# A post-LN decoder layer on one core: every engine's hand-written order of steps replaced by another, PSUM turns in other banks

## Chip, cores, metric

One core of one Trainium2 chip runs the whole kernel. The metric is the device time of that core in microseconds (us); three runs of the kernel before are given.

## What is computed

64 sequences of 128 tokens with 512 features go through one decoder layer: self-attention, cross-attention and a linear layer on fp8-rounded data, each added to its input and layer-normed.

```python
x = _layernorm(x + _L0_attn_ref(x, Wqkv, q_norm_w, k_norm_w, Wo))     # 16 heads of 32; rmsnorm of q and k, rope,
                                                                      # causal softmax, @ Wo
x = _layernorm(x + _L0_xattn_ref(x, ctx, ctx))                        # 8 "heads" of 16 token rows: scores are
                                                                      # 512x512 (features x features), softmax
x = _layernorm(x + _L0_ffn_ref(x, weight))                            # blocks of 128 scaled to fp8 e4m3 and back,
                                                                      # weights too, then x @ weight.T
```

## The kernel before

One batch is one sequence, a tile of 128 tokens by 512 features. The work on a batch is cut into named steps. Five engines run them: TensorE (PE), VectorE (DVE), ScalarE (ACT), GpSimd (POOL) and SyncE (SP), which issues every DMA. Nothing is scheduled at run time: for each engine a table written out by hand (`SP_STEPS`, `POOL_STEPS`, `ACT_STEPS`, `DVE_STEPS`, `PE_STEPS`, L178 to L231) gives the order. An entry `name:k@stage` is part k of a step; in slot t the engine does it for batch t - stage. A slot is one pass through the table, so some six batches are in flight at once: the self-attention of one batch, the cross-attention of earlier ones, the linear layer of a still earlier one. Slots of an engine are its own; engines meet only by semaphores. The stage is therefore partly a name: `ld_x:0@0` and `ld_x:0@1` differ in which slot of SP holds them, not in the batch that comes next.

`LAST` is the highest stage of all tables. The first `LAST + 3` slots and the last ones are written out (unrolled); the others run in a hardware loop (`Fori`, two slots per round, so that double buffers have fixed addresses).

PE's steps in the order of one batch: `x_T` (transpose x), `proj_q/k/v` (each four parts of three matmuls: the operand is split into a high part `lin_h` and a low part `lin_l`, and high x high, high x low, low x high are summed), `parts_T` (transposed q and k), `self_scores` (for the row maximum), `self_shift_T`, `self_scores_T`, `self_pv`, `proj_o`; then `context_T`, 32 `cross_scores` (for the maximum) into two PSUM banks `mx`, `cross_shift_T`, 32 `cross_scores_T` into two banks `st`, 8 `cross_pv` into bank `pv`, `group_T`, `back_T`; then `quant_T` and `ffn`.

For these DVE does `cross_max` (one for each of the 32 `cross_scores`, of which PE may be two ahead), `self_max`, `self_shift`, `cross_shift`, `rope_terms`, `self_recip` and `self_norm`, `cross_norm`, the sums `add_self`, `add_cross`, `add_ffn`, `layernorm` and the low parts `xT_low`, `oT_low`, `xdT_low`. ACT does `probs` (exp of each `cross_scores_T`, again two ahead at most), `self_probs`, `self_stack`, `context_out`, `group_out`, `part_high` and the high parts `xT_high`, `oT_high`, `xdT_high`. POOL does `quant_unit` and `quant_round`, `layer_rstd`, `mask`, `rope_sum`, `part_low`, `query_low`, `mean_square`, `context_rest`. The row maxima of the cross-attention go as a shift through DRAM: `cross_shift_T` (PE), `cross_shift_out` (ACT), `st_sh2` and `ld_sh2` (SP, L413 and L420), and `cross_scores_T:0` and `:16` wait for the load.

All results of PE other than these go into three shared PSUM banks. `BANK` (L235) gives each kind of result, a "turn", its bank. Turns of one bank follow each other in PE's order: a turn waits (`before`) until the one ahead of it in the same bank has been read out, which the reader says by `bank_free`. `full` and `freed` are the points at which a turn is written or read out.

`lin_h` and `lin_l` exist once, and the three linear layers (q, k and v together; o; ffn) use them in turn. Nothing in the code before makes the writer of `lin_h` wait until the layer ahead has been read; the order of the tables does it.

Of the kernel before, what the change touches and what calls it, by code (L numbers as in the profile page):

```python
# [5 lines left out]
def post_ln_decoder_kernel(nc, x, ctx_in, wqkv, q_norm_w, k_norm_w, wo, wffn, cos_t, sin_t, out):  # L6
# [52 lines left out]
    with es:  # L59
# [127 lines left out]
        ACT_STEPS = steps("""
            probs:4@4 self_stack:2@1 probs:5@4 probs:6@4 probs:7@4 self_stack:3@1 probs:8@4 probs:9@4
            context_out:0@3 probs:10@4 probs:11@4 probs:12@4 probs:13@4 probs:14@4 xdT_high:0@5
            context_high:0@2 probs:15@4 xT_high:0@0 cross_shift_out:1@4 query_high:0@2 group_out:0@4  # L190
            square:0@0 self_shift_out:0@1 context_high:1@2 probs:16@4 square:1@0 part_high:0@0
            probs:17@4 probs:18@4 probs:19@4 value:0@0 self_probs:0@1 probs:20@4 self_probs:1@1
            probs:21@4 probs:22@4 self_probs:2@1 probs:23@4 self_probs:3@1 probs:24@4 probs:25@4
            self_stack:0@0 probs:26@4 probs:27@4 cross_shift_out:0@3 probs:28@4 probs:29@4 probs:30@4
            probs:31@4 part_high:1@0 oT_high:0@1 group_out:1@4 self_stack:1@0 probs:0@3 probs:1@3
            probs:2@3 probs:3@3""")
        DVE_STEPS = steps("""
            layernorm:1@5 quant_scale:0@5 add_self:0@2 quant_magic:0@5 cross_max:22@4 cross_max:23@4
            self_max:0@1 cross_max:24@4 cross_max:25@4 cross_max:26@4 cross_max:27@4 cross_max:28@4
            cross_max:29@4 xdT_low:0@5 self_max:1@1 cross_max:30@4 cross_max:31@4 self_max:2@1  # L200
            cross_shift:1@4 layernorm:0@2 cross_max:0@3 xT_low:0@0 add_ffn:0@5 self_max:3@1
            layernorm:2@5 cross_max:1@3 self_shift:0@1 cross_max:2@3 rope_terms:0@0 cross_max:3@3
            cross_max:4@3 cross_max:5@3 cross_max:6@3 cross_max:7@3 cross_max:8@3 rope_terms:1@0
            cross_max:9@3 cross_max:10@3 cross_max:11@3 cross_max:12@3 cross_max:13@3 cross_max:14@3
            cross_max:15@3 cross_shift:0@3 self_recip:0@1 self_recip:1@1 self_recip:2@1 self_recip:3@1
            cross_max:16@3 self_norm:0@1 cross_max:17@3 cross_norm:0@4 oT_low:0@1 cross_max:18@3
            cross_norm:1@4 cross_max:19@3 add_cross:0@4 cross_max:20@3 cross_max:21@3""")
        PE_STEPS = steps("""
            proj_o:3@2 context_T:0@3 cross_scores_T:5@4 cross_scores_T:6@4 cross_pv:0@4
            cross_scores_T:7@4 parts_T:3@1 cross_scores_T:8@4 cross_scores:23@4 self_scores:0@1  # L210
            cross_scores_T:9@4 cross_pv:1@4 cross_scores_T:10@4 cross_scores:24@4 cross_scores:25@4
            cross_scores_T:11@4 self_scores:1@1 cross_scores_T:12@4 cross_scores:26@4 self_scores:2@1
            cross_scores:27@4 cross_scores_T:13@4 cross_scores_T:14@4 cross_scores:28@4 quant_T:0@5
            cross_scores:29@4 cross_scores_T:15@4 cross_pv:2@4 cross_scores:30@4 cross_scores:31@4
            ffn:0@5 ffn:1@5 ffn:2@5 ffn:3@5 x_T:0@0 cross_shift_T:1@4 cross_scores:0@3 cross_pv:3@4
            self_scores:3@1 cross_scores:1@3 proj_q:0@0 proj_q:1@0 proj_q:2@0 proj_q:3@0
            cross_scores:2@3 proj_k:0@0 proj_k:1@0 self_shift_T:0@1 proj_k:2@0 cross_scores:3@3
            proj_k:3@0 cross_scores_T:16@4 cross_scores:4@3 proj_v:0@0 cross_scores_T:17@4
            cross_scores:5@3 cross_scores_T:18@4 cross_scores:6@3 proj_v:1@0 cross_scores:7@3
            proj_v:2@0 cross_scores:8@3 cross_scores_T:19@4 cross_scores:9@3 cross_scores_T:20@4  # L220
            proj_v:3@0 self_scores_T:0@1 cross_pv:4@4 cross_scores:10@3 self_scores_T:1@1
            cross_scores_T:21@4 cross_scores:11@3 cross_scores_T:22@4 self_scores_T:2@1
            cross_scores:12@3 self_pv:0@1 cross_scores:13@3 cross_scores_T:23@4 self_pv:1@1
            self_scores_T:3@1 cross_scores:14@3 cross_scores_T:24@4 cross_scores:15@3
            cross_scores_T:25@4 self_pv:2@1 parts_T:0@0 self_pv:3@1 cross_scores_T:26@4
# [850 lines left out]
```

## Time and profile before

| | us |
|---|---|
| median of 3 runs | 3355.27 |
| lowest, highest | 3353.78, 3358.29 |
| the profiled execution, span | 3353.3 |

| engine | busy us | share |
|---|---|---|
| PE matmul | 3148.0 | 94% |
| PE weight load | 1676.5 | 50% |
| DVE | 2792.0 | 83% |
| ACT | 2093.1 | 62% |
| POOL | 1251.8 | 37% |

The busy shares are even over the whole span except the first and the last tenth. PE's records overlap (a matmul is recorded with its way through the array), so its busy share says little of how full it is; distances between starts say more. The DMA queues move 66 GB/s on the mean and their packets take 21% of the time of the 16 engines.

### The profile page before, as it was taken

What the parts mean: (1) busy time and instruction counts of PE and PEld (TensorE: products, weight loads), DVE (VectorE), ACT (ScalarE), POOL (GpSimd) and SP (SyncE); (2) the same over time, 40 slices, a digit from 0 to 9 for tenths busy, and PEclk for the clock granted to TensorE, in tenths of its full rate; (3) what the DMA queues carried; (4) which work ended last, traced back from release to release, by engine and by line L of the source; (5) the groups of instructions that cost most, each with busy time, mean ns of one, the idle gap of its engine ahead of it and who ended that gap; (6) DMA issues with size and microseconds to landing.
All of it is one profiled execution on the core that took longest, in us unless ns stands there. A gap on an engine that the chain in (4) does not pass through costs nothing.

```text
span 3353.3 us, 79176 instructions
## 1 busy us (share of the span) xinstructions
PE 3148.0 (94%) x22224; PEld 1676.5 (50%) x22224; DVE 2792.0 (83%) x5187; ACT 2093.1 (62%) x3905; POOL 1251.8 (37%) x1623
## 2 busy tenths in 40 slices
PE   1689999999999999999999999999999999999986
PEld 1445555555555555555555555555555555555432
DVE  6368888888888888888888888888888888888874
ACT  0346666666676666666667666666666766666653
POOL 3223334334343333433433333343343433334321
PEclk9789999999999999999999999999999999999997
DMA  2022222222222222222222122222222222222220
GB/s 75 26 62 74 71 67 71 63 72 65 70 73 64 72 64 66 71 63 73 64 70 73 63 71 66 66 71 63 71 66 70 73 63 71 65 66 71 67 64 17
DMA packets 203973, 220.66 MB, mean 66 GB/s; under 512 B 37760, under 2 KB 160640, under 8 KB 203776
## 3 DMA queue, kind: packets, MB, share of 16 engines
q1 hardware_dynamic: 203776, 218.77, 21.4%
q14 instruction: 163, 1.34, 0.1%
q8 instruction: 34, 0.56, 0.1%
HBM read 141.57 MB, written 77.07 MB: 65 GB/s over the span
## 4 chain that ended last, share of the span: by engine, by line
PE 75%; DVE 14%; issue 7%; POOL 2%; ACT 1%; DVEq 1%; DMA 1%; SPq 0%; POOLq 0%; ACTq 0%
PE bank L872 19%; PE mx L985 14%; PE st L1002 13%; PE pv L1014 12%; PE bank L865 5%; PE bank L907 3%; DVE nm L715 3%; PE bank L956 3%; DVE st L776 2%; PE bank L939 2%; PE bank L959 2%; DVE lin_l L743 1%; DVE yout L838 1%; PE bank L923 1%; PE bank L920 1%
## 5 line engine op out<-in xcount | busy, mean ns | idle before, releaser
L715 DVE TENSOR_REDUCE nm<-mx 128x1 f32<-128x512 f32 x2048 | 1355.0, 685 | 219.9 <-PE mx L985 210.2
L559 ACT ACTIVATE pp<-st 128x512 f32<-128x512 f32 x2048 | 1153.0, 597 | 400.9 <-PE st L1002 385.1
L985 PE MATMUL mx<-kst,qst 96*128 96x512 bf16 x2048 | 765.4, 387 | 29.2 <-DVE nm L715 28.8
L1002 PE MATMUL st<-qst,kst 98*128 98x512 f16 x2048 | 739.6, 387 | 6.9 <-DMA qst<-cross_shift 2.6
L1014 PE MATMUL pv<-pp,vT 128*32 128x512 f32 x4096 | 551.2, 610 | 0.0
L985 PEld LDWEIGHTS mx<-kst,qst 96*128 96x128 f16 x2048 | 189.1, 98 | 445.5 <-DVE nm L715 283.1
L872 PE MATMUL bank<-w_h,lin_h 128*128 128x512 f32 x768 | 394.0, 513 | 4.5 <-DVE lin_l L743 4.4
L1002 PEld LDWEIGHTS st<-qst,kst 98*128 98x128 bf16 x2048 | 190.7, 98 | 317.8 <-ACT pp L559 216.6
L490 POOL TENSOR_SCALAR rstd<-mv 128x1 f32<-128x1 f32 x192 | 36.9, 192 | 817.2 <-DVE mv L779 812.1
L872 PE MATMUL bank<-w_l,lin_h 128*128 128x512 f32 x768 | 306.0, 398 | 0.0
L872 PE MATMUL bank<-w_h,lin_l 128*128 128x512 f32 x768 | 305.0, 397 | 0.0
L500 POOL TENSOR_TENSOR qkn<-ropeA,qkn 128x512 f16<-128x512 f32 x128 | 148.4, 1159 | 397.2 <-ACT qkn L581 391.4
L763 DVE RECIPROCAL o<-bank 128x128 f32<-128x128 f32 x256 | 217.1, 910 | 42.8 <-PE bank L959 42.7
L506 POOL TENSOR_SCALAR_AFFINE_SELECT p<-p 128x512 f32<-128x512 f32 x256 | 163.4, 638 | 197.8 <-ACT p L616 197.7
L496 POOL TENSOR_TENSOR ropeA<-ropeA,ropeB 128x512 f32<-128x512 f32 x128 | 163.7, 1279 | 144.9 <-DVE ropeB L755 144.9
L574 ACT ACTIVATE junk<-bank 128x512 bf16<-128x512 f32 x128 | 76.1, 594 | 203.3 <-PE bank L872 203.3
L616 ACT ACTIVATE p<-bank 128x512 f32<-128x512 f32 x256 | 152.6, 596 | 56.1 <-PE bank L939 47.4
L729 DVE TENSOR_REDUCE nm<-bank 128x4 f32<-128x512 f32 x256 | 174.6, 683 | 10.4 <-PE bank L923 10.3
L568 ACT ACTIVATE lin_h<-bank 128x512 fp32r<-128x512 f32 x64 | 38.2, 597 | 221.1 <-PE bank L865 221.1
L907 PE MATMUL bank<-ident,qkn 128*96 128x128 f16 x2048 | 161.9, 223 | 14.4 <-DVE o L763 7.2
L872 PEld LDWEIGHTS bank<-w_h,lin_h 128*128 128x128 f32 x768 | 149.4, 195 | 44.8 <-DVE lin_l L743 5.9
L907 PEld LDWEIGHTS bank<-ident,qkn 128*96 128x96 f16 x2048 | 146.0, 125 | 48.4 <-issue 19.3
(131 smaller groups left out, 5417.6 us busy)
## 6 DMA issues: line engine op xcount, KB each, us to landing
qst<-q_planes SPq DMA_DIRECT2D x640, 64.0 KB, 2.2
kst<-k_planes SPq DMA_DIRECT2D x640, 64.0 KB, 2.2
k_planes<-kpl SPq DMA_DIRECT2D x64, 384.0 KB, 2.6
xb<-x SPq DMA_DIRECT2D x64, 256.0 KB, 2.7
cx<-ctx SPq DMA_DIRECT2D x64, 256.0 KB, 3.3
...
```

The lines of the kernel that those rows point to most:

```text
L496: g_.tensor_tensor(ropeA[:], ropeA[:], ropeB[:], ALU.add).then_inc(s_rope, 1)
L506: g_.affine_select(out=p1[c % 2][:], in_=p1[c % 2][:], compare_op=ALU.is_ge, fill=0.0, base=0, pattern=[[0, HC], [1, P]], channel_multipli ...
L559: a.activation(pp[:, unit % 2, j, :], st[n % 2][:], ACT.Exp, scale=CROSS_SCALE).then_inc(st_free, 1)
L715: v.tensor_reduce(nm2[:, n // 16, n % 16:n % 16 + 1], mx[n % 2][:], AX.X, ALU.max, negate=True)\
L729: v.tensor_reduce(nm1[:, HC * c:HC * (c + 1)], at(f"s1m{c}")[:].rearrange("p (h k) -> p h k", h=HC), AX.X, ALU.max, negate=True).then_inc( ...
L763: v.reciprocal(o1[:, cols], at("pvs")[:, cols]).then_inc(done, 1)
L865: last = t.transpose(dst[:, c * P:(c + 1) * P], src(c), idm[:])
L872: last = t.matmul(at(name)[:], a[:, rows], w[:, part, cols], start=(part == 0 and i == 0), stop=(part == KC - 1 and i == 2))
L907: last = t.transpose(at(name)[0:SROWS, h * P // 2:(h + 1) * P // 2].bitcast(F16), qkn[k][:, 8 * (i % 2) + h, :, :].rearrange("p g d -> p ( ...
L985: t.matmul(mx[n % 2][:], qst[b.i][0:XROWS, h, c * P:(c + 1) * P], kst[b.i][0:XROWS, h, :], start=True, stop=True).then_inc(mx_full, 1)
L1002: t.matmul(st[n % 2][:], kst[b.i][:, h, i * P:(i + 1) * P], qst[b.i][:, h, :], start=True, stop=True).then_inc(st_full, 1)
L1014: last = t.matmul(pv[32 * j:32 * j + 2 * XD, :], vT[b.i][:, i, GH * g + j, :], pp[:, unit % 2, j, :], start=(i == 0), stop=(i == KC - 1))
```

## The change

Every engine does the same steps, in another order. Some stages are renamed, on SP by one or two, so that `LAST` goes from 5 to 7: the loop begins at slot 10 instead of 8, has 26 rounds instead of 27, and the program has 71 slots instead of 69. Eleven turns have another bank. And the three steps that write `lin_h` wait, by a new function `linear_before`, until the linear layer ahead of theirs in PE's order is done. The tables, the banks and the waits after the change, cut to the parts that are spoken of:

```diff
         SP_STEPS = steps("""
-            ld_cx:0@2 ld_qst:1@3 ld_kst:0@3 ld_x:0@0 st_sh2:1@4 ld_sh2:1@4 st_out:0@5 st_qpl:0@2
-            st_sh1:0@1 ld_sh1:0@1 ld_qst:0@2 st_x2:0@2 ld_x2r:0@4 st_sh2:0@3 st_kpl:0@2 ld_sh2:0@3
-            ld_kst:1@2""")
+            st_sh2:0@5 ld_x2r:0@6 st_kpl:0@4 st_out:0@7 st_x2:0@4 st_qpl:0@4 ld_sh2:0@5 ld_kst:0@4
+            ld_qst:0@4 ld_cx:0@3 ld_x:0@1 st_sh1:0@2 st_sh2:1@5 ld_sh1:0@2 ld_sh2:1@5 ld_kst:1@4
+            ld_qst:1@4""")
...
         ACT_STEPS = steps("""
+            part_high:1@1 group_out:1@5 self_stack:1@1 probs:0@4 probs:1@4 context_out:0@3
+            probs:2@4 oT_high:0@2 probs:3@4 probs:4@4 self_stack:2@1 probs:5@4 probs:6@4 probs:7@4
+            probs:8@4 probs:9@4 probs:10@4 self_stack:3@1 probs:11@4 context_high:0@2 xdT_high:0@5
+            probs:12@4 probs:13@4 xT_high:0@0 self_shift_out:0@1 context_high:1@2
...
+            query_high:0@2 probs:25@4 self_probs:3@1 probs:26@4 probs:27@4 self_stack:0@0
+            probs:28@4 cross_shift_out:0@3 probs:29@4 probs:30@4 probs:31@4""")
         DVE_STEPS = steps("""
+            cross_norm:1@5 cross_max:24@4 self_norm:0@2 add_cross:0@5 cross_max:25@4 oT_low:0@2
+            layernorm:1@5 quant_scale:0@5 cross_max:26@4 cross_max:27@4 quant_magic:0@5
+            cross_max:28@4 cross_max:29@4 self_max:0@1 cross_max:30@4 add_self:0@2 cross_max:31@4
+            cross_max:0@3 self_max:1@1 xdT_low:0@5 self_max:2@1 cross_max:1@3 self_max:3@1
+            cross_max:2@3 self_shift:0@1 cross_shift:1@4 xT_low:0@0 cross_max:3@3 cross_max:4@3
+            add_ffn:0@5 cross_max:5@3 cross_max:6@3 layernorm:0@2 cross_max:7@3 cross_max:8@3
...
+            cross_max:17@3 cross_max:18@3 cross_shift:0@3 cross_max:19@3 layernorm:2@5
+            cross_max:20@3 self_recip:0@1 self_recip:1@1 self_recip:2@1 cross_max:21@3
+            cross_norm:0@4 self_recip:3@1 cross_max:22@3 cross_max:23@3""")
         PE_STEPS = steps("""
+            self_pv:3@2 cross_scores_T:28@5 cross_shift_T:0@4 cross_scores_T:29@5
+            cross_scores:21@4 cross_scores_T:30@5 group_T:0@5 cross_scores_T:31@5 cross_pv:6@5
+            cross_pv:7@5 cross_scores:22@4 parts_T:1@1 cross_scores:23@4 group_T:1@5
+            cross_scores:24@4 cross_scores_T:0@4 back_T:0@5 cross_scores:25@4 cross_scores_T:1@4
+            context_T:0@3 cross_scores_T:2@4 parts_T:2@1 cross_scores_T:3@4 cross_scores_T:4@4
+            parts_T:3@1 cross_scores_T:5@4 cross_scores:26@4 cross_scores_T:6@4 proj_o:0@2
...
+            ffn:0@5 ffn:1@5 ffn:2@5 x_T:0@0 ffn:3@5 cross_scores:3@3 cross_scores:4@3
+            self_shift_T:0@1 cross_pv:2@4 cross_shift_T:1@4 cross_scores_T:14@4
+            cross_scores_T:15@4 proj_q:0@0 proj_q:1@0 cross_scores:5@3 cross_pv:3@4
...
         BANK = {
+            "xT": 1, "q": 1, "k": 2, "v": 1, "tqk0": 1, "tqk1": 1, "tqk2": 2, "tqk3": 1, "s1m0": 2,
+            "s1m1": 0, "s1m2": 1, "s1m3": 0, "m1T": 0, "s1t0": 0, "s1t1": 0, "s1t2": 1, "s1t3": 1,
+            "pvo": 0, "pvs": 2, "wo": 0, "vT": 2, "mT0": 1, "mT1": 0, "o2T0": 1, "o2T1": 2, "o2N": 1,
             "xdT": 2, "ffn": 2}
...
+        LINEARS = (("proj_q", "v"), ("proj_o", "wo"), ("ffn", "ffn"))
+
+        def linear_before(name, b):
+
+            opens = [(i, stage, turn) for i, (step, k, stage) in enumerate(PE_STEPS) if k == 0
+                     for first, turn in LINEARS if step == first]
+            own = [turn for _, _, turn in opens].index(name)
+            for back in range(1, len(opens) + 1):
+                _, stage, turn = opens[own - back]
+                ahead = opens[own][1] - stage - (back > own)
+                if b.rnd is not None or 0 <= b.b + ahead < BATCH:
+                    return [full(turn, b, ahead)]
+            return []
...
             def xT_high(b, _):
+                for point in linear_before("v", b):
+                    act.wait_ge(*point)
                 act.wait_ge(*full("xT", b))
...
             def oT_high(b, _):
+                for point in linear_before("wo", b):
+                    act.wait_ge(*point)
...
             def xdT_high(b, _):
+                for point in linear_before("ffn", b):
+                    act.wait_ge(*point)
```

## Rows read from the trace of the kernel before

**Rows 1.** The page: engines with busy us and share; the chain that ended last.
```profile
PE 3148.0 (94%) x22224; PEld 1676.5 (50%) x22224; DVE 2792.0 (83%) x5187; ACT 2093.1 (62%) x3905; POOL 1251.8 (37%) x1623
PE 75%; DVE 14%; issue 7%; POOL 2%; ACT 1%; DVEq 1%; DMA 1%; SPq 0%; POOLq 0%; ACTq 0%
```

**Rows 2.** Tile lin_l, whole run and three stretches: count, durations, first and last start us.
```profile
L743 DVE TENSOR_TENSOR lin_l<-bank,lin_h x64: 680/681/692, 71.8 to 3130.2; 128x512 fp32r<-128x512 f32 x64
...
L743 DVE TENSOR_TENSOR lin_l<-bank,lin_h x20: 680/681/682, 1505.7 to 2442.0; 128x512 fp32r<-128x512 f32 x20
...
L743 DVE TENSOR_TENSOR lin_l<-bank,lin_h x4: 681/681/681, 323.8 to 468.9; 128x512 fp32r<-128x512 f32 x4
...
L743 DVE TENSOR_TENSOR lin_l<-bank,lin_h x2: 681/681/681, 1554.2 to 1604.2; 128x512 fp32r<-128x512 f32 x2
```

**Rows 3.** Stage 1500 to 1549.1 with its clock; PE timeline: start us, us, what.
```profile
1500.00:1549.10 49.10, 48.62 (x355) 25.93 (x347) 43.45 (x82) 33.09 (x64) 19.11 (x25) 1.00 0.22 68
...
1508.25 0.39 PE L872 MATMUL bank<-w_l,lin_h 128*128 128x512 f32 x1
1508.48 0.39 PE L872 MATMUL bank<-w_h,lin_l 128*128 128x512 f32 x1
...
1519.16 1.06 PE L1014 MATMUL pv<-pp,vT 128*32 128x512 f32 x8
1520.15 0.39 PE L985 MATMUL mx<-kst,qst 96*128 96x512 bf16 x1
1520.38 0.39 PE L939 MATMUL bank<-qs,ks 98*128 98x128 f16 x4
```

**Rows 4.** Timeline around `self_shift_T`, 1504 to 1512: PE, DVE, POOL.
```profile
1511.68 0.22 PE L930 MATMUL bank<-ident,sh 128*32 128x128 f16 x1 [0.48 <-DVE sh L739]
...
1509.06 1.37 DVE L784 TENSOR_SCALAR yout<-yout,mv,rstd 128x512 f32<-128x512 f32 x1 [0.44 <-POOL rstd L492]
...
1508.99 1.16 POOL L540 TENSOR_TENSOR qpl<-x,qpl 128x512 f16<-128x512 f32 x1
```

**Rows 5.** The jumps: waits, DVE and ACT timeline, instruction queue of 1480 to 1578.6.
```profile
DVE x L784 <- issue: 48.3, 26, 2.0
...
1490.42 0.55 DVE L784 TENSOR_SCALAR x<-x,mv,rstd 128x512 f32<-128x512 f32 x1 [2.03 <-issue]
...
1488.02 1.16 ACT L559 ACTIVATE pp<-st 128x512 f32<-128x512 f32 x2 [0.55 <-PE st L1002]
...
q14 instruction: 5, 0.04, 0.1%
```

**Rows 6.** SP's timeline from 1499 on; landing of the stores; first user on PE.
```profile
1528.69 0.36 SPq L413 DMA_DIRECT2D cross_shift<-sh2T  x1
1529.31 0.41 SPq L373 DMA_DIRECT2D k_planes<-kpl  x1
1530.29 0.29 SPq L420 DMA_DIRECT2D qst<-cross_shift  x1
...
cross_shift<-sh2T SPq DMA_DIRECT2D x128, 8.0 KB, 1.4
...
1534.64 0.60 PE L1002 MATMUL st<-qst,kst 98*128 98x512 f16 x2
```

**Rows 7.** DVE's timeline of 1526 to 1535.
```profile
1526.55 3.39 DVE L763 RECIPROCAL o<-bank 128x128 f32<-128x128 f32 x4 [0.49 <-PE bank L959]
...
1534.00 0.24 DVE L799 RECIPROCAL r<-bank 128x16 f32<-128x16 f32 x1
1534.27 0.43 DVE L802 TENSOR_TENSOR yq<-bank,r 128x256 f32<-128x256 f32 x1
```

**Rows 8.** ACT: `context_out` (ns min/median/max); timeline of 1525 to 1529.
```profile
L640 ACT ACTIVATE vT<-bank x64: 583/602/612, 170.7 to 3256.2; 128x512 f32<-128x512 f32 x64
...
1525.94 1.02 ACT L600 ACTIVATE qs<-bank 96x1024 f16<-96x1024 f16 x1 [0.37 <-PE bank L907]
1528.19 0.27 ACT L646 ACTIVATE sh2T<-bank 32x128 f16<-32x128 f16 x1 [0.26 <-PE bank L991]
```

More of the change, by code:

```diff
@@ L178, in post_ln_decoder_kernel @@
         SP_STEPS = steps("""
-            ld_cx:0@2 ld_qst:1@3 ld_kst:0@3 ld_x:0@0 st_sh2:1@4 ld_sh2:1@4 st_out:0@5 st_qpl:0@2
-            st_sh1:0@1 ld_sh1:0@1 ld_qst:0@2 st_x2:0@2 ld_x2r:0@4 st_sh2:0@3 st_kpl:0@2 ld_sh2:0@3
-            ld_kst:1@2""")
+            st_sh2:0@5 ld_x2r:0@6 st_kpl:0@4 st_out:0@7 st_x2:0@4 st_qpl:0@4 ld_sh2:0@5 ld_kst:0@4
+            ld_qst:0@4 ld_cx:0@3 ld_x:0@1 st_sh1:0@2 st_sh2:1@5 ld_sh1:0@2 ld_sh2:1@5 ld_kst:1@4
+            ld_qst:1@4""")
         POOL_STEPS = steps("""
-            quant_unit:0@5 quant_round:0@5 quant_round:1@5 quant_round:2@5 layer_rstd:0@2
@@ L184, in post_ln_decoder_kernel @@
-            context_rest:0@2 layer_rstd:2@5 query_low:0@2 mean_square:0@0 rope_sum:0@0 mean_square:1@0
-            part_low:0@0 context_rest:1@2 mask:0@1 mask:1@1 rope_sum:1@0 mask:2@1 mask:3@1 part_low:1@0
-            layer_rstd:1@4""")
+            quant_round:0@5 quant_round:1@5 quant_round:2@5 layer_rstd:0@2 context_rest:0@2
+            mean_square:0@0 rope_sum:0@0 mean_square:1@0 part_low:0@0 layer_rstd:2@5 mask:0@1
+            context_rest:1@2 mask:1@1 rope_sum:1@0 mask:2@1 mask:3@1 query_low:0@2 part_low:1@0
@@ L187, in post_ln_decoder_kernel @@
+            layer_rstd:1@4 quant_unit:0@4""")
         ACT_STEPS = steps("""
[L188 to L196, printed above, removed]
-        DVE_STEPS = steps("""
[L198 to L207, printed above, removed]
@@ L208, in post_ln_decoder_kernel @@
-        PE_STEPS = steps("""
[L209 to L225, printed above, removed]
-            cross_scores_T:27@4 cross_pv:5@4 cross_shift_T:0@3 cross_scores_T:28@4 cross_scores_T:29@4
-            group_T:0@4 cross_scores_T:30@4 cross_scores:16@3 cross_scores_T:31@4 cross_pv:6@4
-            cross_scores:17@3 cross_pv:7@4 cross_scores:18@3 cross_scores:19@3 parts_T:1@0 group_T:1@4
-            proj_o:0@1 cross_scores:20@3 cross_scores_T:0@3 cross_scores_T:1@3 back_T:0@4 parts_T:2@0
-            proj_o:1@1 cross_scores_T:2@3 cross_scores:21@3 proj_o:2@1 cross_scores_T:3@3
-            cross_scores:22@3 cross_scores_T:4@3""")
@@ new lines, in post_ln_decoder_kernel @@
+            part_high:1@1 group_out:1@5 self_stack:1@1 probs:0@4 probs:1@4 context_out:0@3
+            probs:2@4 oT_high:0@2 probs:3@4 probs:4@4 self_stack:2@1 probs:5@4 probs:6@4 probs:7@4
+            probs:8@4 probs:9@4 probs:10@4 self_stack:3@1 probs:11@4 context_high:0@2 xdT_high:0@5
+            probs:12@4 probs:13@4 xT_high:0@0 self_shift_out:0@1 context_high:1@2
+            cross_shift_out:1@4 probs:14@4 probs:15@4 group_out:0@4 square:0@0 self_probs:0@1
+            probs:16@4 probs:17@4 square:1@0 part_high:0@0 probs:18@4 probs:19@4 probs:20@4
```

18 lines of the change are left out of this document (added), and 3 rows, old and new, of the table BANK.

## The prediction

> **What bounds the kernel now.** I read the page first. TensorE (PE) is busy in 94% of the span and carries 75% of the chain that ended last, VectorE (DVE) 14% [rows 1]. A busy PE is not a full one, so the next view is the pace: the instruction at L743 (`xT_low`) runs once for each batch, so the distance between two of them is one period. All 64 give (3130.2 - 71.8)/63 = 48.55 us; inside the hardware loop 20 of them give (2442.0 - 1505.7)/19 = 49.28 us; in the unrolled slots ahead of it four of them give (468.9 - 323.8)/3 = 48.37 us [rows 2]. The kernel is 71.8 us of start, 63 periods, and 223 us from the last L743 to the end.
>
> How full is PE in a period? I take the distance from one start to the next where nothing waits. A linear matmul costs 0.23 us, a scores matmul 0.22, a `cross_pv` 0.99 plus 0.09 ahead of it [rows 3]. In the same way, from the PE rows of one period, a block of four transposes costs 0.44, `parts_T` 0.45, `self_pv` 0.67, `self_scores` 0.44, `self_scores_T` 0.22, a shift transpose 0.15. A period has 60 linear matmuls (14.0), 64 scores (14.1), 8 `cross_pv` (8.7), 6 transpose blocks (2.6), 4 each of `parts_T`, `self_pv`, `self_scores`, `self_scores_T` (7.1), 3 shifts (0.5): 47.0 us. The granted clock of the stretch is 1.00, the level of 2.4 GHz [rows 3]. So 49.28 is a floor of 47.0 plus 2.3 us of waits. The change keeps every step, so the floor stays, and the question is only which waits go and which come.
>
> **What the change removes.** (a) `self_shift_T` stands behind `proj_k:1`. PE arrives 0.75 us too early: the shift on DVE stands behind `add_ffn` and `layernorm:2`, which waited for POOL and took 1.37 us instead of 0.55 because POOL's `query_low` ran beside it [rows 4]. In the new order `self_shift` stands well ahead of `add_ffn` and `self_shift_T` behind `ffn:3` and two scores; it is early by about 1 us. Gain 0.75 a period. (b) Once in two slots DVE jumps back to the head of its loop: 2.03 us of idle with nothing awaited, 26 such, 48.3 us in all. ACT's jump falls between two `probs` at 1488.02 and costs nothing [rows 5]. DVE's jump makes PE late by the difference of 50.0 and 48.5 us that neighbouring L743 show [rows 2], 0.7 a period. The instruction queue loads 5 blocks in two periods [rows 5]. Counted over the trace's instructions, its loads come after every 128 instructions of an engine, and these 5 are all DVE's: DVE's body of the loop (291 instructions) lay over four such blocks, ACT's (336) over three, and only the engine with four reloads. LAST goes from 5 to 7, so the loop begins at slot 10 and the bodies move. Counting the two more unrolled slots from the tables, I estimate that DVE's body comes to lie on three blocks and ACT's, by 11 instructions, on four: the reload goes over to ACT. (c) `group_T:0` waits 0.25 for `cross_shift_out:0` today; in the new order it does so no more.
>
> The Trainium skill (Runtime: NRT & Kernel Launch, section Instruction fetch mechanics) says that a taken branch whose target has left the window of resident blocks waits for a fetch. That agrees with the idle of DVE in the trace; without this rule only the estimate of which engine pays next would be missing.
>
> **What it adds.** I walk the new PE table at floor pace, from the start of `self_pv:3` at 0: `cross_scores_T:28` 0.58, `cross_shift_T:0` 0.80, T30 1.39, `cross_pv:7` 3.45, `group_T:1` 5.34, `cross_scores_T:0` 6.00, `back_T` 6.22, `context_T` 7.09, `parts_T:2` 7.75, `proj_o:0` 9.56.
>
> (d) `cross_scores_T:0` needs `ld_sh2:0`. On ACT `self_stack:0` (1.02) and `probs:28` stand ahead, so `cross_shift_out:0` (0.27) ends at 1.75 [rows 8] and `st_sh2:0` starts at 1.95. On SP it was followed by one other DMA and then `ld_sh2:0`, 1.60 us behind; now five stand between (`ld_x2r`, `st_kpl`, `st_out`, `st_x2`, `st_qpl`), and one unblocked DMA follows another after 0.62 us [rows 6], or somewhat more where, as for `ld_x2r` and `ld_sh2`, it has two waits. So `ld_sh2:0` is issued at about 1.95 + 6 x 0.68 = 6.0. Its landing is not shown; the store of the same 8 KB lands after 1.4, and today PE uses it 4.35 us after the issue without waiting for it [rows 6]. I take 1.6, near the store's: T0 at 7.6 instead of 6.0, `back_T` at 7.8 instead of 6.22. Bounds for the wait: 1.2 (DVE's chain, next) to 2.5.
>
> (e) `back_T` also needs the DVE chain: three `self_recip` from 0.71 on (0.82 to 0.88 each), `cross_max:21` (a `cross_max` keeps DVE 0.6), `cross_norm:0`, `self_recip:3`, `cross_max:22`, `:23`, `cross_norm:1` [rows 7]: 0.71 + 2.5 + 0.6 + 0.67 + 0.82 + 1.2 + 0.75 = 7.3. Today 9.2 us of PE work lie over this chain, then 6.2. It is 1.15 late, beside (d) and not added to it. Together with 0.25 at T30, which waits for `probs:28`, (d) and (e) give 1.6.
>
> (f) `parts_T:2` now takes the bank that `context_T` has just filled: transposes 0.60, `context_out` 0.60 [rows 8], two hand-overs, 1.3 us where PE has 0.66 of work. Wait 0.65 (bounds 0.6 and 0.9). Behind it PE's whole queue stands.
>
> (g) T3 to T6 follow at 0.2 to 0.5 us while ACT, at 0.5 a `probs`, also has `context_out`, `oT_high` and `self_stack:2`: 0.3 (bounds 0 and 0.6).
>
> (h) ACT's reload, 3.0 us from branch to work as on DVE, stands ahead of `part_high:1` and `group_out:1`; `group_T:1`, `cross_norm:1`, `back_T` follow at 9.05 instead of 7.8: 1.25 in two slots, 0.6 a period (bounds 0 and 1.3).
>
> (i) The three waits for the preceding linear layer: `xT_high` now waits for `ffn:3`, which follows `x_T` at once. ACT gets going at 24.0 by the new table, `xT_low` ends 1.5 us later, and `proj_q` comes at 25.55 with `self_shift_out` and `context_high:1` queued behind on ACT, neither needed within 1 us: nothing. `oT_high` waits for a `proj_v` and `xdT_high` for a `proj_o` that are over: nothing; from below 0, from above 0.2 if ACT is late.
>
> One rule speaks about (e). The row first: `layernorm:2` took 1.37 us, until 0.28 after `query_low` had ended [rows 4]. The Trainium skill (SBUF — State Buffer, section SBUF: two separate sides) calls the port pair of VectorE and GpSimd an exclusive lock held for a whole instruction. In the new order `layernorm:2` stands just ahead of the `self_recip`s and again meets `query_low`. By my walk it gets free 0.1 us before they can start; were it later by the whole 0.8, (e) would give 7.3 + 0.7 and only draw level with (d). So the sum is the same by the one and by the other.
>
> **Sum.** New slot: 47.0 + 0.3 (the small waits left) + 1.6 + 0.65 + 0.3 = 49.85, in the loop 50.45 with (h). Loop: 52 slots x (50.45 - 49.28) = +61. Two slots move from the loop to straight code: 2 x (49.85 - 49.28) = +1. About five full slots outside: 5 x (49.85 - 48.37) = +7. Start and end keep their chains. Against the profiled execution of 3353.3 (median of the runs 3355.3, 2 us more): 3355 + 69 = 3424.
>
> **Rivals.** R1, faster: `ld_sh2:0` lands early enough that (e) alone sets `back_T`, ACT's reload is hidden, and (g) is nothing. Slot 47.0 + 1.2 + 0.65 = 48.85 with none of the small waits left: 52 x -0.43 + 5 x 0.5 = -20, 3335. It decides at a `ld_sh2:0` issued under 4 us after `st_sh2:0`. For it: (a) and (b) are sure gains of 1.4. Against: five issues at 0.62 or more. Chance 0.19. R2, nothing to measure: ACT pays no reload and (d) is nearer 1.2 than 1.6: 49.4 in all slots, 3355 + 6 = 3361. Chance 0.08. R3: as forecast but without (h): 52 x 0.57 + 8 = +38, 3393. Chance 0.18. R4: both reloads remain, DVE's ahead of `cross_norm:1` where no cover is: another 0.6 a period, 3455. Chance 0.08. That the change doesn't do what it says can't be: the tables are the program. My forecast has 0.47.
>
> **Numbers.** Differences under 0.2% (7 us) can't be told from none. Faster 0.19 (R1), same 0.08 (R2), slower 0.73. The range runs from R1's end to R4's, 3335 to 3455.
>
> **What would show it.** L743 spacing of about 49.9 and 51 us in turn; at `cross_scores_T:0` a PE wait for the DMA from the shift's scratch; at `parts_T:2` (L907) one for ACT's L640; `self_shift_T` without a wait; DVE's 2 us idle of "issue" gone and one like it on ACT. Wrong would be: spacing under 49.3, or no wait at L1002 for a DMA. Then SP's five DMAs are cheaper than these rows say, or the walk sets two waits side by side that are one.

## The result and the profile after

The changed kernel takes 3645.6 us (median of 4 runs, 3638.0 to 3648.2), the kernel before 3355.3: a ratio of 1.086, interval 1.084 to 1.088, 290 us slower. The profiled execution is 3642.2 us long. The forecast was 3424.

Below, from the page of the kernel after: engines, granted clock (in 40 slices), the two instruction queues (loads, MB, share), the chain by engine.

```profile
PE 3220.9 (88%) x22224; PEld 1706.6 (47%) x22224; DVE 2813.1 (77%) x5187; ACT 2103.5 (58%) x3905; POOL 1249.0 (34%) x1623
...
PEclk9999999999999999999999999999999999999998
...
q8 instruction: 265, 4.34, 0.5%
q14 instruction: 162, 1.32, 0.1%
...
PE 76%; issue 9%; DVE 5%; SPq 3%; DMA 3%; ACT 3%; POOL 1%; ACTq 0%; DVEq 0%; POOLq 0%
```

Against [rows 1], PE has 73 us more of busy time for the same 22224 matmuls, and "issue", an engine waiting for nothing the profile shows, rose from 7% to 9%. The line that the prediction did not use is q8, the instruction queue of PE: 265 loads of 16 KB, where the page of before has 34. q14, with the other engines' loads of 8 KB, has nearly as many as before (162, then 163).

The pace, as in [rows 2], is now read at L765 (the same `xT_low`): the whole run, a stretch in the loop, one ahead of it.

```profile
L765 DVE TENSOR_TENSOR lin_l<-bank,lin_h x64: 684/692/693, 71.7 to 3422.3; 128x512 fp32r<-128x512 f32 x64
...
L765 DVE TENSOR_TENSOR lin_l<-bank,lin_h x43: 691/692/692, 676.6 to 2994.3; 128x512 fp32r<-128x512 f32 x43
...
L765 DVE TENSOR_TENSOR lin_l<-bank,lin_h x4: 692/692/692, 259.9 to 410.3; 128x512 fp32r<-128x512 f32 x4
```

Outside the loop a slot takes (410.3 - 259.9)/3 = 50.1 us, 0.3 over the forecast of 49.85. Inside it takes (2994.3 - 676.6)/42 = 55.2, against 50.45. So some 5 us a slot arise only in the loop, where 0.6 were forecast. The 50.1 comes near the walk's sum by two errors that nearly cancel (below, under the floor).

PE's rows with the waits of the whole run (engine, line, releaser: us, times, longest), and both engines' rows with "issue":

```profile
PE bank L978 <- issue: 93.5, 25, 4.8
...
PE st L1024 <- DMA qst<-cross_shift: 57.9, 39, 2.2
PE bank L887 <- ACT o L580: 42.2, 27, 2.7
PE bank L929 <- ACT vT L660: 32.1, 62, 0.8
ACT qkn L598 <- issue: 31.4, 11, 4.1
PE mx L1007 <- issue: 25.9, 25, 1.8
```

L978 is `self_pv`, the first thing behind PE's branch: 25 stalls of 3.7 us with nothing awaited, one at each of the 25 jumps back. In each round a second one of 1.0 us follows some 3 us later, at a `cross_scores` (L1007). L1024 is the forecast wait of `cross_scores_T:0` for the shift's DMA, L929 that of `parts_T:2` for `context_out`. DVE's row of 26 stalls of 1.9 us in the mean [rows 5] is gone, and ACT has one in its place, at `part_high:1` (L598). `self_shift_T` (L952) has no row any more.

Two neighbouring slots of the loop, as in [rows 3] (us of window; busy PE, PEld, DVE, ACT, POOL; granted clock; DMA), then the timelines of PE and ACT behind the branch of the next round:

```profile
1471.80:1525.60 53.80, 50.52 (x347) 26.74 (x351) 41.85 (x78) 32.27 (x61) 19.07 (x25) 0.94 0.20 64
1525.60:1580.60 55.00, 48.34 (x358) 25.82 (x350) 44.56 (x83) 33.26 (x62) 19.07 (x25) 1.00 0.20 62
```

```profile
1580.59 0.66 PE L978 MATMUL bank<-p,va 128*32 128x128 f32 x8 [3.69 <-issue]
...
1581.60 0.61 PE L1024 MATMUL st<-qst,kst 98*128 98x512 f16 x1
...
1591.58 0.38 PE L1024 MATMUL st<-qst,kst 98*128 98x512 f16 x1
...
1589.10 0.63 ACT L598 ACTIVATE qkn<-ropeA 128x512 f16<-128x512 f32 x1 [2.58 <-issue]
```

A stall of 3.69 us; behind it the scores matmul takes 0.61 us where it takes 0.38 ten us later: the clock's lower level, 1.2 GHz, granted after the idle (0.50 from 1580.7 to 1587.4, 1.00 on both sides of it). Where a slot's mean clock is 0.94, such stretches are in it. ACT's stall of 2.58 follows in the same slot.

Last, the term (d), SP's queue and the waiting scores matmul, as in [rows 6]:

```profile
1527.69 0.35 SPq L429 DMA_DIRECT2D cross_shift<-sh2T  x1
...
1531.16 0.74 SPq L448 DMA_DIRECT2D q_planes<-qpl  x1
1532.31 0.28 SPq L436 DMA_DIRECT2D qst<-cross_shift  x1
...
1534.57 0.39 PE L1024 MATMUL st<-qst,kst 98*128 98x512 f16 x1 [1.79 <-DMA qst<-cross_shift]
```

The load is issued 4.62 us behind the store (forecast: 4.1), its user starts 2.26 behind the issue and had waited 1.79 (forecast: 1.6).

### The profile page after: what moved, and what is told of

It reads as the page before. It is cut to its first block, busy times and chain, and to the rows that moved or that the text cites. A ratio compares the mean times of both kernels' runs of the same rounds, so it can differ in the third digit from the quotient of the medians.

```text
span 3642.2 us, 78580 instructions
## 1 busy us (share of the span) xinstructions
PE 3220.9 (88%) x22224; PEld 1706.6 (47%) x22224; DVE 2813.1 (77%) x5187; ACT 2103.5 (58%) x3905; POOL 1249.0 (34%) x1623
## 4 chain that ended last, share of the span: by engine, by line
PE 76%; issue 9%; DVE 5%; SPq 3%; DMA 3%; ACT 3%; POOL 1%; ACTq 0%; DVEq 0%; POOLq 0%
PE bank L894 25%; PE st L1024 13%; PE mx L1007 11%; PE pv L1036 11%; PE bank L887 4%; PE bank L929 3%; DMA qst<-cross_shift 2%; PE bank L978 2%; PE bank L942 2%; PE bank L981 2%; PE bank L945 2%; PE bank L961 2%; DVE x L813 1%; ACT vT L660 1%; SPq L448 1%
## 5 line engine op out<-in xcount | busy, mean ns | idle before, releaser
L575 ACT ACTIVATE pp<-st 128x512 f32<-128x512 f32 x2048 | 1168.5, 597 | 689.1 <-PE st L1024 501.9
L1024 PE MATMUL st<-qst,kst 98*128 98x512 f16 x2048 | 795.4, 404 | 67.6 <-DMA qst<-cross_shift 57.9
L1007 PE MATMUL mx<-kst,qst 96*128 96x512 bf16 x2048 | 789.3, 391 | 37.2 <-issue 25.9
L1036 PE MATMUL pv<-pp,vT 128*32 128x512 f32 x4096 | 561.7, 633 | 3.2 <-ACT pp L575 3.2
L894 PE MATMUL bank<-w_h,lin_h 128*128 128x512 f32 x768 | 402.9, 525 | 6.3 <-DVE lin_l L765 4.7
L1024 PEld LDWEIGHTS st<-qst,kst 98*128 98x128 bf16 x2048 | 196.6, 100 | 417.6 <-ACT pp L575 202.7
L1007 PEld LDWEIGHTS mx<-kst,qst 96*128 96x128 f16 x2048 | 195.8, 98 | 409.5 <-issue 266.0
L498 POOL TENSOR_SCALAR rms<-ssq 128x1 f32<-128x1 f32 x128 | 24.5, 191 | 801.1 <-ACT junk L592 800.9
L785 DVE RECIPROCAL o<-bank 128x128 f32<-128x128 f32 x256 | 225.0, 920 | 90.9 <-PE bank L981 90.9
L929 PE MATMUL bank<-ident,qkn 128*96 128x128 f16 x2048 | 166.4, 227 | 57.1 <-ACT vT L660 32.1
L929 PEld LDWEIGHTS bank<-ident,qkn 128*96 128x96 f16 x2048 | 147.9, 128 | 126.9 <-issue 53.3
L978 PE MATMUL bank<-p,va 128*32 128x128 f32 x2048 | 110.6, 289 | 95.8 <-issue 93.5
L1036 PEld LDWEIGHTS pv<-pp,vT 128*32 128x32 f32 x4096 | 91.6, 112 | 177.6 <-issue 87.1
```

The source lines that it names most:

```text
L575: a.activation(pp[:, unit % 2, j, :], st[n % 2][:], ACT.Exp, scale=CROSS_SCALE).then_inc(st_free, 1)
L785: v.reciprocal(o1[:, cols], at("pvs")[:, cols]).then_inc(done, 1)
L894: last = t.matmul(at(name)[:], a[:, rows], w[:, part, cols], start=(part == 0 and i == 0), stop=(part == KC - 1 and i == 2))
L929: last = t.transpose(at(name)[0:SROWS, h * P // 2:(h + 1) * P // 2].bitcast(F16), qkn[k][:, 8 * (i % 2) + h, :, :].rearrange("p g d -> p ( ...
L978: last_v = t.matmul(at("pvo")[HD * j:HD * (j + 1), cols], va[b.i][:, HC * c + j, :], p1[c % 2][:, j, :], start=True, stop=True)
L1007: t.matmul(mx[n % 2][:], qst[b.i][0:XROWS, h, c * P:(c + 1) * P], kst[b.i][0:XROWS, h, :], start=True, stop=True).then_inc(mx_full, 1)
```

## The experiments

Each compares with the kernel before on the same chip (3353.7 to 3357.9 in these sets). The waits put in ahead of an engine's first slot are on a semaphore that has long been raised; two such waits make one instruction, so a loop over 129 in place of one wait gives 64 instructions more. Where they delay the start, the first `xT_low` shows by how much, and I take that off.

**Moving the bodies.** e1, the changed kernel with 64 more instructions on PE, nothing changed in the body:

```
-            pe.wait_ge(u_done, 1)
+            for _ in range(129):
+                pe.wait_ge(u_done, 1)
```

> The changed kernel with 64 satisfied waits put ahead of TensorE's first slot, so that its loop body of 1583 instructions lies 64 instructions further on; nothing inside the body differs. Theory (the position of the body decides): in the changed kernel TensorE's instruction queue loads 9 blocks of 16 KB in each of the 26 rounds and the pair of slots takes 109.3 us, where two slots outside the loop take 100.2. Moved on by 64, the body lies over one block fewer, the loads inside the loop go (some 35 to 40 in all, from 265), and a slot in the loop takes about 50.1 + 0.6 (ScalarE's own reload) = 50.7 us: 3645 - 52 x 4.0 = 3437 us, between 3415 and 3460. Rival (the new order or the new banks cost this inside the loop only, through a wait that needs the steady state): nothing of the order is touched, so 3645 +- 10 us and 109 us per round.

3544.5 us (ratio 1.055, 1.053 to 1.057), 40 loads on q8, no "issue" row for `self_pv` (L979 there). The start was delayed by 7.0 us, so the reload of PE, with what follows from it, costs 101 + 7 = 108 us, 4.2 in each of 26 rounds, half of what I had expected: moving the body stops the reload, and its price had been set at twice its size. What was left over pointed at ACT. The waits, two slots:

```profile
ACT qkn L598 <- issue: 48.2, 20, 2.6
...
PE bank L888 <- ACT o L580: 35.6, 28, 1.7
```

```profile
1340.20:1393.90 53.70, 50.75 (x355) 27.30 (x351) 43.07 (x81) 32.60 (x62) 19.12 (x25) 0.94 0.21 63
1393.90:1446.40 52.50, 49.84 (x355) 26.78 (x348) 43.01 (x81) 32.94 (x62) 19.10 (x25) 0.97 0.21 64
```

e4, the same and 30 more instructions on ACT (`for _ in range(61)`):

> The first of these kernels with 30 satisfied waits ahead of ScalarE's first slot as well: ScalarE's body of 334 instructions then lies over three blocks of 128, not four. Theory (term h): the 2.7 to 4.5 us at ScalarE's branch falls to 0.3, which gives 1.2 us in two slots: 26 x 1.2 = 32 us below the kernel with the 64 waits alone, about 3405 us if that one takes 3437. Rival (ScalarE has slack at its branch and the reload costs nothing): the same time as that kernel within 0.2%.

3484.4 us (1.039, 1.035 to 1.044), 60 below e1: 2.3 us a round, twice the forecast 1.25. The direct part is the row of L888 above, `group_T:1` waiting for `group_out` 35.6 us in 28 times, 1.3 each; that row is gone in e4. The rest I put down to the clock: in e1 both slots above are under 1.00, in e4 most slots take 50.9 us and have 1.00, and the mean granted clock of the whole run rises from 0.957 to 0.973.

e3, the kernel before with 40 more instructions on DVE:

> The kernel before with 40 satisfied waits ahead of VectorE's first slot: its body of 291 instructions then lies over three blocks of 128, not four. Theory (terms b and the rule of four blocks in the prediction): the 2.0 us at VectorE's branch falls to about 0.3 as on GpSimd and SyncE, 5 loads per round go, and what it cost the path, 0.7 us in each slot of the loop, goes with it: 3355 - 54 x 0.7 = 3318 us, between 3305 and 3335. Rival (the path waits for something else at that place, or other waits take it over): within 0.2% of 3355 though the loads go. Second rival (the position does not decide): the branch still takes 2 us.

3313.9 us (0.987, 0.985 to 0.988), 42.9 below the kernel before; forecast by term (b): 38. q14 falls to 33 loads, DVE's 26 stalls are gone, and all slots of the loop take 48.5 us, but one. Three slots, and PE's timeline in the middle one:

```profile
550.00:598.00 48.00, 47.52 (x347) 25.60 (x346) 42.47 (x80) 32.40 (x61) 19.12 (x25) 1.00 0.23 69
598.00:653.00 55.00, 51.24 (x349) 27.16 (x349) 43.02 (x81) 32.78 (x61) 19.08 (x25) 0.94 0.21 62
653.00:702.00 49.00, 48.47 (x350) 26.32 (x349) 43.27 (x82) 32.77 (x62) 19.11 (x25) 1.00 0.23 69
```

```profile
603.25 0.77 PE L873 MATMUL bank<-wo_h,lin_h 128*128 128x512 f32 x1 [3.28 <-issue]
603.82 0.63 PE L873 MATMUL bank<-wo_l,lin_h 128*128 128x512 f32 x1
```

There, in one round, PE reloaded in the order of before too: 9 loads more (43 on q8, not 34), a stall of 3.28 us behind the branch at 599.46, matmuls of 0.63 us instead of 0.40 after it, and a slot 6.3 us longer than its neighbours. So the reload is not bound to the changed order. It also shows that PE's place alone does not decide: e3 leaves PE's body where the kernel before has it.

**Where does PE reload?** If the body's place decides, the kernel before must be brought to do it. e2 and e5, before with 222 and 233 more instructions on PE:

> The kernel before with 222 satisfied waits ahead of TensorE's first slot: its body of 1581 instructions moves to where, in 256s, that of the changed kernel lies. Theory (position): 9 blocks per round for each of 27 rounds, some 280 loads instead of 34, and 7 to 8 us more per round, as in the changed kernel: 3355 + 27 x 7.6 + some us for the waits themselves = 3565 us, between 3530 and 3600. Rival (the order and the banks of the changed kernel are what costs): only the waits themselves, 3355 to 3370 us, and no load inside the loop.

> The kernel before with 233 satisfied waits ahead of TensorE's first slot: its body now begins at 130 of 256, exactly where that of the changed kernel does (the 222 of the run before put it at 119, where nothing was reloaded). Theory (position alone decides whether TensorE reloads): 9 blocks in each of 27 rounds, some 280 loads in all, and per round what the changed kernel paid beyond its copy moved by 64, (3645.6 - 3544.5 + 10 for the 64 waits) / 26 = 4.3 us: 3357 + 23 for the waits themselves + 27 x 4.3 = 3495 us, between 3450 and 3530. Rival (the changed kernel reloads by something of its own order, such as how far its front end runs ahead): no load in the loop and 3380 us as with 222.

3379.6 and 3381.5 us, 35 loads each, none in the loop; the first L743 came 24 and 25 us late, which is all the difference. My theory fell in this form, although with 233 the body lay where that of the changed kernel does. Mended, it was tried with e9 (22 more), e12 and e13 (the changed kernel with 24 and 245 more), e14 and e16 (before with 245 and 5 more):

> The kernel before with 22 satisfied waits ahead of TensorE's first slot: its body of 1581 instructions then begins at 175 and branches at 219, counted in 256s of the profiled instructions. Theory, mended after the runs with 222 and 233: what decides is whether TensorE fetches one more block before it reaches its branch. The loads seen in straight-line code fall at 163 to 220 of 256 in all kernels; in the changed kernel the last one fell 13 instructions ahead of the branch in the first round of the loop, and every later round reloaded; in the kernel before it would fall about at the branch (once it fell 9 ahead, and that round reloaded), and with 222 and 233 it falls behind the branch. With 22 it falls some 20 to 45 instructions ahead in each round: 9 loads in each of 27 rounds, and 3357 + 3 for the waits + 27 x 4.3 = 3476 us, between 3430 and 3510. Rival (the reload belongs to the changed kernel's order, not to where the body lies): 3360 us and no load in the loop.

> The changed kernel with 24 satisfied waits ahead of TensorE's first slot, not 64. In it TensorE runs on for 20 instructions behind its branch and then stalls 3.5 to 3.8 us for the next block, so a block ends 20 instructions into the body; 24 further on, that border lies ahead of the body, which then touches 7 blocks and not 8. Theory (a body that touches 8 blocks can reload, one of 7 can not): some 40 loads, no stall, 3645 - 101 - some us, near 3545. Rival (only a shift that is far enough, or the timing at the branch, stops it): 265 loads and 3645 us.

> The changed kernel with 245 satisfied waits ahead of TensorE's first slot: the body starts 11 instructions earlier in its block than in the changed kernel (245 = 256 - 11), so it still touches 8 blocks, with its branch some 15 instructions into the eighth. Theory (8 blocks in the changed kernel's order reload): some 265 loads in all and 3645 + 25 to 35 us for the waits. Rival (the reload of the changed kernel hangs on the exact place at which its branch lies in the eighth block): about 40 loads and 3545 + 30 us.

> The kernel before with 245 satisfied waits ahead of TensorE's first slot: its body starts some 12 instructions ahead of the border of a block and touches 8 blocks, with the branch some 35 into the eighth. With none, 222, 233 and 22 waits it did not reload. Theory (the same as for the changed kernel: 8 blocks, and the branch far enough in the eighth that one more block is asked for first): 9 loads per round and 3357 + 25 + 27 x 4.3 = 3500 us. Rival (in this order the ninth block is not asked for before the branch, wherever the branch lies): 35 loads and 3382 us.

> The kernel before with 5 satisfied waits ahead of TensorE's first slot. Of the changed kernel's four places two reloaded (branch at 176 and 200 of 256) and two did not (165 and 240); of six places of the kernel before none did (163, 174, 186, 219 and, twice, 197), but for one round at 197. Theory (one more block is fetched before the branch, if the branch lies far enough behind the border of a block, and only while the body's start lies ahead of that border; 197 is just short of it in this order): at 202 some or all of the 27 rounds reload, each for 4 to 6 us: 3358 + 27 x 5 = 3490 us if all do. Rival (nothing of this order brings the reload on): 3358 us and 34 loads.

The table gives where the branch at the body's end lies among the instructions of PE in the trace, counted from the first and modulo 256 (a 16 KB load is 256 of them).

| kernel | more instructions | branch at | q8 loads | us |
|---|---|---|---|---|
| after | 0 | 176 | 265 | 3645.6 |
| after (e12, one run) | 24 | 200 | 265 | 3698.9 |
| after (e1) | 64 | 240 | 40 | 3544.5 |
| after (e13, one run) | 245 | 165 | 41 | 3575.4 |
| before (e2) | 222 | 163 | 35 | 3379.6 |
| before (e5) | 233 | 174 | 35 | 3381.5 |
| before (e14, one run) | 245 | 186 | 35 | 3384.2 |
| before | 0 | 197 | 34 | 3355.3 |
| before (e16, one run) | 5 | 202 | 34 | 3360.1 |
| before (e9) | 22 | 219 | 34 | 3357.4 |

In the changed kernel it goes by the place: the same body reloads at two places and not at two others. The waits that move the body also delay PE's start (by 7 us in e1), and the two were not tried apart. e13, less the 27 us by which its start is late, is 3548.5, where e1 less its 7 is 3537.5. e12 is dearer than the kernel after: its second stall in a round is 2.5 us and not 1.0.

```profile
PE bank L979 <- issue: 89.3, 25, 3.9
...
PE bank L982 <- issue: 63.3, 25, 3.0
```

```profile
975.80:1027.00 51.20, 48.46 (x353) 26.19 (x352) 43.45 (x81) 32.72 (x61) 19.08 (x25) 1.00 0.22 67
1027.00:1087.00 60.00, 51.35 (x346) 26.39 (x346) 43.01 (x81) 32.80 (x61) 19.06 (x25) 0.91 0.19 57
```

In the kernel before none of six places brought it on, save the one round of e3. e12's expectation (a body that touches 7 blocks can't reload) was wrong, and so were those of e9, e13, e14 and e16. One thing goes with it: in after and e12 a load begins 0.0 to 0.5 us ahead of 47 of the 52 branches, and 0.2 to 0.8 us behind the other five; in e3's one round it begins 0.95 ahead. Where nothing reloads, none begins less than 2.4 us ahead of a branch. That looks like one block more fetched just ahead of the branch, in the place of one that the body's start still needs; it is argued, not shown. What makes PE fetch it in one order and not in the other at like places stays open.

**The forecast waits.** With the reloads of PE and ACT away, what is left of the change can be tried by itself. e6 is e4 with the load directly behind its store:

```
-            st_sh2:0@5 ld_x2r:0@6 st_kpl:0@4 st_out:0@7 st_x2:0@4 st_qpl:0@4 ld_sh2:0@5 ld_kst:0@4
+            st_sh2:0@5 ld_sh2:0@5 ld_x2r:0@6 st_kpl:0@4 st_out:0@7 st_x2:0@4 st_qpl:0@4 ld_kst:0@4
```

> The changed kernel without reloads (64 waits on TensorE, 30 on ScalarE: 3484 us) and ld_sh2:0 directly behind st_sh2:0 on SyncE, where five other steps lie between. Theory (term d: the first transposed scores of the new batch wait 1.5 to 2 us for that load, behind five DMAs, and TensorE's clock falls after that wait in some slots): the wait falls to nothing, back_T then waits up to 1.2 us for VectorE's chain (term e), the slot falls from 50.9 to 49.9 to 50.4, and the slots of 52 to 55 us with a low clock go (0.5 us a slot in the mean): 3484 - 64 x 1.1 = 3414 us, between 3380 and 3450. Rival (that wait ends by the store's and load's own latency, or the other five steps now come late): 3484 +- 10 us.

3389.9 us (1.010, 1.008 to 1.012), 94.5 below e4: better than the middle of my range. First e4: the wait's row, two slots, PE in the slower one; then e6: `cross_scores_T:0` with `back_T` behind it, and the spacing:

```profile
PE st L1026 <- DMA qst<-cross_shift: 98.3, 63, 2.7
```

```profile
1383.80:1434.70 50.90, 48.17 (x359) 25.80 (x351) 43.01 (x81) 32.84 (x62) 19.11 (x25) 1.00 0.22 65
868.30:923.10 54.80, 52.33 (x356) 28.63 (x348) 43.10 (x81) 33.06 (x62) 19.12 (x25) 0.91 0.20 61
```

```profile
877.05 0.61 PE L1026 MATMUL st<-qst,kst 98*128 98x512 f16 x1 [1.58 <-DMA qst<-cross_shift]
877.45 1.06 PE L889 MATMUL bank<-ident,yq 128*128 128x128 f32 x4
```

```profile
1448.31 0.38 PE L1026 MATMUL st<-qst,kst 98*128 98x512 f16 x1
1449.38 0.63 PE L889 MATMUL bank<-ident,yq 128*128 128x128 f32 x4 [0.70 <-DVE yq L825]
```

```profile
L766 DVE TENSOR_TENSOR lin_l<-bank,lin_h x47: 691/692/692, 668.4 to 2969.9; 128x512 fp32r<-128x512 f32 x47
```

The DMA's wait of 98.3/63 = 1.56 us is gone; `back_T` now waits 0.70 for DVE, which is term (e) come to light behind (d), as forecast. The slot falls from 50.9 to (2969.9 - 668.4)/46 = 50.03. And the slots of 52 to 55 us are gone: in e4 they had a clock of 0.91 to 0.97; right behind the wait the transposes took 1.06 us, in e6 0.63, in some slots and not in others with like waits. So the wait cost 0.85 us a slot by itself and in the mean of the loop another 0.5 by the clock.

e7 is e4 with `"vT": 0` in place of 2:

> The changed kernel without reloads (3484 us) and the turn vT in bank 0, where the kernel before had it, not in bank 2 just ahead of the third parts_T. Theory (term f): the 0.6 to 0.7 us for which parts_T:2 waits for context_out in each slot goes, and nothing else is late there: 3484 - 64 x 0.65 = 3442 us, between 3425 and 3460. Rival (proj_o:0, whose turn is in bank 0 too, then waits for context_out or self_norm in its place): 3484 +- 10 us.

3478.3 us (1.038, 1.035 to 1.040), 6 below e4, within the scatter of both. The wait left its place:

```profile
PE st L1026 <- DMA qst<-cross_shift: 102.1, 63, 3.0
...
PE st L1026 <- ACT pp L576: 29.9, 116, 0.7
```

The row of `parts_T:2` for `context_out` (32.5 us in 62 in e4) is not there any more, and PE waits 29.9 us for ACT's exponentials, 116 times, where e4 has 4.8 us in 15. So ACT holds PE up at this place with the bank or without.

e11 is e6 with `back_T:0` behind `cross_scores_T:2`, four steps later; e15 is e11 with `oT_low:0` ahead of `add_cross:0` on DVE:

> The changed kernel without reloads and with ld_sh2:0 forward (3390 us), and back_T four steps later on TensorE, behind cross_scores_T:2. Theory (term e: back_T waits 0.86 us for VectorE's chain; term f: parts_T:2 waits 0.7 us for context_out): in the new place VectorE is ready, and back_T's own 0.44 us covers part of the wait behind it: 50.03 - 0.86 - 0.4 = 48.8 us a slot, 3390 - 64 x 1.2 = 3313 us, between 3300 and 3340. Rival (ScalarE's exponentials, which run late in the same stretch, take the place of both waits, as they did when vT changed its bank): 3390 to 3375 us.

> The changed kernel without reloads, ld_sh2:0 forward and back_T later (3398 us), with VectorE's oT_low ahead of add_cross, where it stood behind it. In the kernel of 3398 us the waits of back_T and parts_T:2 were gone and proj_o:0 waited 0.8 to 1.1 us for oT_low, which stood behind add_cross, which waits for back_T. Theory (VectorE's order of these two hands the wait on): proj_o:0's wait goes and the slot falls from 50.1 to 49.2: 3398 - 64 x 0.9 = 3340 us, between 3325 and 3365. Rival (VectorE's chain is late as a whole, or ScalarE's oT_high is): 3398 +- 10 us.

3398.5 (1.013, 1.011 to 1.015) and 3476.7 us (1.036, 1.035 to 1.038). Neither gained. The waits of e11 first, then of e15:

```profile
PE bank L896 <- DVE lin_l L796: 43.5, 62, 0.8
```

```profile
PE mx L1009 <- DVE nm L738: 78.4, 80, 2.2
...
PE bank L931 <- DVE x L832: 73.8, 60, 1.3
...
DVE lin_l L796 <- ACT lin_h L642: 79.1, 64, 2.5
```

In e11 `proj_o:0` waits for `oT_low`, which stands behind `add_cross`, which waits for `back_T`. In e15 `parts_T:3` waits for `add_cross` (L832 ends the turn of `back_T` in its bank) and PE for `cross_max` (L738), for `oT_low` itself waits 1.2 us for ACT's `oT_high` in each slot (L796; 4.2 us in all in e11) and holds up DVE's queue. I read this as one chain through PE, DVE and ACT that is late at this place in all three orders (e6, e11, e15); no run takes it away.

**Parts on the kernel before.** e8 is e3 with `self_shift_T` alone moved:

```
-            cross_scores:2@3 proj_k:0@0 proj_k:1@0 self_shift_T:0@1 proj_k:2@0 cross_scores:3@3
+            cross_scores:2@3 proj_k:0@0 proj_k:1@0 proj_k:2@0 cross_scores:3@3 self_shift_T:0@1
```

> The kernel before with VectorE's 40 waits (3314 us) and self_shift_T two steps later on TensorE, behind proj_k:2 and cross_scores:3. Theory (term a alone): the wait of 0.48 us for self_shift and what follows from it, 0.75 us in each slot, goes, as self_shift's result is there 1.1 us before it is asked for: 3314 - 60 x 0.75 = 3269 us, between 3260 and 3290. Rival (proj_v:0, which needs the same bank, waits for self_shift_out instead): 3314 +- 7 us or slower.

3283.7 us (0.978, 0.977 to 0.980): the fastest kernel of this study, 30 below e3 and 74 below the kernel before. The rival fell. The slot went from 48.5 to (2964.2 - 659.8)/48 = 48.0 us: the wait of 0.48 in [rows 4] went and nothing came in its place. The 0.27 that I had added for what follows from it did not.

e10 is e8 with the three waits for the preceding linear layer and 90 more instructions on ACT:

> The kernel of 3284 us (before, 40 waits on VectorE, self_shift_T later) with the changed kernel's waits of xT_high, oT_high and xdT_high for the preceding linear layer added to its own order, and with 90 satisfied waits ahead of ScalarE's first slot so that its longer body does not come to lie over a fourth block. Theory (term i): the preceding linear layer has ended 3 us and more before each of these copies, so the waits cost nothing: 3284 +- 8 us. Rival (a copy comes later, and the linear layer behind it on TensorE too): 0.3 us or more in each slot, 3304 us or more.

3290.2 us (0.981, 0.979 to 0.983), 6.5 more. All of it lies in the start and the end; the slots are the same:

```profile
L765 DVE TENSOR_TENSOR lin_l<-bank,lin_h x64: 680/681/692, 77.8 to 3065.4; 128x512 fp32r<-128x512 f32 x64
```

```profile
L744 DVE TENSOR_TENSOR lin_l<-bank,lin_h x64: 680/681/692, 72.8 to 3059.9; 128x512 fp32r<-128x512 f32 x64
```

e10 above, e8 below: 2987.6 and 2987.1 us from first to last, with the first 5.0 later. The waits cost nothing in the order of before; in that of after this was not tried.

## Why the prediction was wrong

The side was right, the size was not: 3646 against 3424, and over the end of the range. Half of the miss is a reload that the prediction gave to no engine, PE's; the other half are sizes. By steps:

- **(a), (b), (c).** (a) is confirmed by e8 with 0.5 instead of 0.75. (b) is confirmed: DVE's reload went, as the changed kernel's profile shows, and e3 puts it at 43 us, 38 by the forecast (e3's own trace still has the one round with PE's reload). (c): no wait of `group_T:0` in the rows after.
- **The step that failed** is in (b) and (h): "these 5 are all DVE's ... the reload goes over to ACT". It asked of DVE and ACT where their bodies come to lie, and not of PE. The sum has no term for PE's own queue: it had no load in the stretch that the rows showed, and nothing was asked of it after the change. But with the two slots more ahead of the loop and the new table, PE loads 9 blocks in each round, stalls 3.7 and 1.0 us, and runs on at the lower clock. Cost: 108 us (e1), half the miss.
- **(h)** was right in kind and in engine (ACT's stall at `part_high:1`, 48.2/20 = 2.4 us in e1) and half its size: 2.3 us a round and not 1.25 (e4). That is 60 us where the sum had 0.6 x 52 = 31. Its direct part was 1.3; the rest I put down to the clock behind it, which e1 and e4 do not show apart from other waits.
- **(d) and (e)**: the wait for the DMA came at its step and in its size, 1.56 us in the mean without the reloads, against 1.6, and (e) was there behind it with 0.70. What was left out is that the clock could fall behind a wait of this length: e4's loop has (2949.5 - 689.1)/44 = 51.4 us in the mean where its undisturbed slots have 50.9; 0.5 x 52 = 26 us. The first and last L766 of that stretch in e4:

```profile
L766 DVE TENSOR_TENSOR lin_l<-bank,lin_h x45: 690/692/692, 689.1 to 2949.5; 128x512 fp32r<-128x512 f32 x45
```

- **(f), (g)**: `parts_T:2` waits 32.1/62 = 0.5 us, forecast 0.65. (g) was forecast at 0.3, and e4 has 4.8 us in the whole run; e7 shows that when the one goes the other comes, so they are not two costs to be added. A wait that the walk lacked is that of `parts_T:1` for `cross_norm:0`, whose turn is ahead of it in the bank (0.4 us, the last row below).
- **The floor** was set too low, and this is the fourth part of the miss. The e4 slot of 50.9 us shown above (1383.8 to 1434.7, granted clock 1.00) has these waits of PE and no others:

```profile
PE st L1026 <- DMA qst<-cross_shift: 1.5, 1, 1.5
PE bank L931 <- ACT vT L661: 0.6, 1, 0.6
PE bank L931 <- DVE yq L825: 0.4, 1, 0.4
```

 That is 2.5 us of waits, less than the 2.85 that the sum had, and 48.4 of the rest, where the sum had 47.0. The order of before has the same: e8 lists no wait of PE in two slots that take 96.0 us together (1508.3 to 1604.3). So its 49.28 was not 47.0 and 2.3 of waits, and the changed kernel's slot, built up from 47.0 and compared with a measured 49.28, came out too low: 50.9 - 49.85 = 1.05, and 1.05 x 52 = 55 us. Outside the loop the same two errors nearly cancel: 50.1 us there (260.0 to 310.1) hold 2.1 of waits and 48.0 of the rest, against 2.85 and 47.0. That the walk came within 0.3 of it was luck. Which steps cost more than the distances that the prediction took was not taken apart.
- **(i)**: nothing, as forecast, in the order of before (e10).

The four terms (PE's reload, ACT's, the clock behind (d), the floor less the waits) make 108 + 29 + 26 + 55 = 218 of the 222 us. They don't lie wholly apart, since a stall that comes earlier takes some of a later wait with it.

Of the rivals, R1 hung on a load issued under 4 us behind its store; it was 4.6, and e6, where it is 1.7, still is not faster than before. R4 had two reloads in the loop, but DVE's and ACT's. The prediction also said that `layernorm:2` meets `query_low` again; it had no weight in the sum, and it did not come: `layernorm:2` (L806 in the kernel after) takes 0.53 to 0.55 us in all 64 batches, where [rows 4] have 1.37. The Trainium skill (Runtime: NRT & Kernel Launch, section Instruction fetch mechanics) gives the rule for every engine and names PE as the one with the largest store; I had used it for the two whose loads I saw. The same section counts the resident window of a branch as two pages of 16 KiB. PE's body of 1581 instructions, more than six loads of 16 KB, runs in the kernel before without a load in the loop, so for PE the measurement decides against a window of two.
